# A four-layer kernel: fusion stage reordered with two further products a batch, a convolution moved, chunk products parted

## The reference

```python
q = short_conv_silu(hidden @ Wq, conv_q_w)          # causal convolution of 4 taps, then silu; k and v alike
beta = sigmoid(hidden @ Wb)
# delta rule in chunks of 32 tokens; q, k l2-normed, v and kb = k scaled by beta
attn = -(kb @ k^T) * strict_lower                   # per chunk, 32 x 32
for i in range(1, 32):                              # inverse of (1 - attn), row by row
    attn[i, :i] += attn[i] @ attn[:, :i]
u, w = (attn + eye) @ v, (attn + eye) @ kb
# scan over the 16 chunks:
a_loc = (q_i @ k_i^T) * incl_lower
u_i = u_i - w_i @ S;  o_i = q_i @ S + a_loc @ u_i;  S = S + k_i^T @ u_i
# multi-scale causal convolutions of 3, 15 and 31 taps on v, mixed per head and over channels
ms_out = (concat(conv3, conv15, conv31) @ kernel_mix_w) @ channel_mixer_w
# fusion
feat = concat(hidden, mean|ms_out|, mean|delta_out|, mean|v|)          # 128 + 3 x 4
logits = gelu(feat @ fusion_w1 + b1) @ fusion_w2 + b2                  # 3 per head
wts = softmax(logits)
o = wts0 * ms_out + wts1 * delta_out + wts2 * v
o = o * rsqrt(mean(o * o) + 1e-5) * o_norm_w                           # per head
out = o @ Wo
```

## Time and profile before

| | us |
|---|---|
| median of 3 runs (lowest, highest) | 2881.85 (2876.45, 2889.88) |
| profiled execution | 2890.78 |
| its span | 2889.2 |
| PE busy / DVE busy / ACT busy | 2125.6 / 1844.0 / 1167.1 |
| chunk inputs, 2109.7 to 2303.7 | 194.0 |
| solve and convolution, to 2409.9 | 106.2 |
| chunk products, to 2513.9 | 104.0 |
| serial scan, to 2542.2 | 28.3 |
| fusion, to 2680.3 | 138.1 |

### The profile page before, as it was taken

The page is one execution under the profiler, slowest core; times in us unless marked ns, Lnnn a source line. Parts: engine busy times, 40 slices in busy tenths (PEclk is TensorE's granted clock), DMA queues, the critical chain, the costliest instruction groups (busy, mean ns, idle before and its releaser), DMA issues. The chain is left out here.

```text
span 2889.2 us, 44054 instructions
## 1 busy us (share of the span) xinstructions
PE 2125.6 (74%) x15996; PEld 1090.1 (38%) x15996; DVE 1844.0 (64%) x2951; ACT 1167.1 (40%) x2397; POOL 426.7 (15%) x575
## 2 busy tenths in 40 slices
PE   4476778732538768888868766997778797678798
PEld 3011113421328612222235211886533344555454
DVE  6688887656844387878624588332555495856565
ACT  3699994310002136666643322233433101135433
POOL 3000000000551122222210341113500000000100
PEclk9788889855769969999977777998989799867799
DMA  8512110000345512222100000221112312200000
GB/s 289 103 23 44 22 22 1 14 9 0 105 142 154 147 31 39 51 48 39 27 13 0 21 31 9 98 91 41 42 53 75 102 70 71 67 4 1 22 1 30
DMA packets 146759, 155.28 MB, mean 54 GB/s; under 512 B 53136, under 2 KB 122338, under 8 KB 146586
## 3 DMA queue, kind: packets, MB, share of 16 engines
q1 hardware_dynamic: 131936, 119.71, 16.1%
q0 software_dynamic: 12928, 25.47, 3.6%
q10 hardware_dynamic: 1728, 7.87, 0.7%
HBM read 87.29 MB, written 68.55 MB: 54 GB/s over the span
## 5 line engine op out<-in xcount | busy, mean ns | idle before, releaser
L786 DVE TENSOR_REDUCE a_nmax<-a_first 128x2 f32<-128x1024 f32 x256 | 307.3, 1219 | 87.7 <-PE a_first L883 71.2
L381 ACT ACTIVATE a_E<-a_scores,a_nmax 128x512 f32<-128x512 f32 x512 | 343.3, 726 | 21.7 <-DVE a_nmax L340 21.4
L864 ACT ACTIVATE a_E<-a_scores 128x512 f32<-128x512 f32 x512 | 278.2, 597 | 159.3 <-PE a_scores L897 141.8
L340 DVE TENSOR_REDUCE a_nmax<-a_scores 128x2 f32<-128x1024 f32 x256 | 300.3, 1217 | 37.0 <-PE a_scores L398 35.5
L398 PE MATMUL a_scores<-a_Vh,a_Kh 48*128 48x512 bf16 x512 | 113.7, 461 | 132.4 <-ACT a_E L381 101.4
L897 PE MATMUL a_scores<-a_Qh,a_Kh 51*128 51x512 bf16 x512 | 143.1, 398 | 51.5 <-ACT a_E L864 39.1
L409 PE MATMUL a_out<-a_E,a_QS 128*32 128x512 f32 x1024 | 165.9, 727 | 2.7 <-DVE a_QS L350 2.6
L883 PE MATMUL a_first<-a_Kh,a_Qh 48*128 48x512 bf16 x512 | 122.2, 419 | 34.6 <-DVE a_nmax L786 23.9
L1885 PE MATMUL a_ps_q<-a_yT,a_selI 32*128 32x512 f32 x128 | 101.7, 885 | 57.5 <-DVE a_state L1943 34.1
L910 PE MATMUL a_out<-a_E,a_V 128*32 128x512 f32 x1024 | 143.0, 632 | 0.4 <-POOL a_V L720 0.2
L398 PEld LDWEIGHTS a_scores<-a_Vh,a_Kh 48*128 48x128 bf16 x512 | 24.8, 96 | 304.2 <-ACT a_E L381 218.3
(11 more groups left out here) (464 smaller groups left out, 4644.4 us busy)
## 6 DMA issues: line engine op xcount, KB each, us to landing
f_up<-in_L_up SPq DMA_DIRECT2D x32, 256.0 KB, 2.9
slots<-zeros ACTq DMA_DIRECT2D x12, 640.0 KB, 15.4
a_rows_k<-a_parts SPq DMA_DIRECT2D x16, 384.0 KB
a_Kh<-a_rows_k SPq DMA_DIRECT2D x16, 384.0 KB, 5.8
a_Vh<-a_rows_v SPq DMA_DIRECT2D x16, 384.0 KB, 9.4
a_Qh<-a_rows_q SPq DMA_DIRECT2D x32, 192.0 KB, 4.6
a_Kh<-a_rows_k SPq DMA_DIRECT2D x32, 192.0 KB, 5.1
f_xe<-slots SPq DMA_DIRECT2D x40, 128.0 KB, 2.0
```

Of the source, the lines that this page charges most:

```text
L340: v.tensor_reduce(nmax[:, rd % 2, r1, :, q], ps_s[u % 3][:], AX.X, ALU.max, negate=True).then_inc(S["max_ready"], 1)
L381: m = a.activation(E[:, u % NE, x], ps_s[u % 3][:, x], ACT.Exp, bias=nmax[:, rd % 2, r1, x, q:q + 1], accum_out=Z[:, rd % 2, r1, x, q:q + 1])
L786: v.tensor_reduce(out, ps_f[u % 2][:], AX.X, ALU.max, negate=True).then_inc(S["max_ready"], 1)
L864: a.activation(E[:, u % NE, x], ps_s[x][:], ACT.Exp, scale=SCALE).then_inc(S["exp_ready"], 1)
```

## The change

- `attention3`: G stays allocated through `chunk_scan3`; `eye` is loaded with the first ring loads.
- `chunk_inputs3`: `quads` is parted into `quads_a` and `quads_l`, `masks` into `mask_a` and `mask_l`. The two `sums` products go to 32 partitions each (0 to 31, 32 to 63) instead of adding up in 8; `spread` reads the reciprocals from these two groups of 32.
- `solve_and_convolve3`: PE convolves 6 batches (`CONV3`); the turned copies MT are done by ACT.
- `chunk_scan3`: the 15 early taps of batches 6 and 7 are done here, two taps a step (`taps_of`); ACT issues the loads of q, all at the start; `ps_c` has one buffer instead of two.
- `fusion3`: all engines follow one schedule (`turns`), in which a batch passes through six turns of the loop; branches and o are held for three batches. The two hidden products from the features read rows 0 to 31 and 32 to 63 of FT, which holds the features twice. Two products of the identity by XT are added a batch, into `ps_h`, where the next products overwrite them. The weighted sum isn't divided by the sum of the weights; the square of that sum scales the 1e-5 in the norm instead.
- The weights of layer 0 are freed before layer 2.

```diff
@@ chunk_inputs3, tensor @@
                     for n in range(2):
-                        m = pe.matmul(ps_b[0:8, :], hm8[:, n], sq[:, n], start=(n == 0), stop=(n == 1))
+                        m = pe.matmul(ps_b[32 * n:32 * n + 32, :], hm[:], sq[:, n], start=True, stop=True)
...
-                        m = pe.matmul(ps_n[:, n], sp8[:, n], rs[:], start=True, stop=True)
+                        rows = slice(32 * n, 32 * n + 32)
+                        m = pe.matmul(ps_n[:, n], sp8[rows], rs[rows], start=True, stop=True)
...
+                def quads_a(b):
                     pe.wait_ge(S["kb_ready"], b + 1)
+                    pe.wait_ge(S["a_masked"], b)
+                    quads(b, ps_a, kb[:], y[:, b % 2, 1]).then_inc(S["a_done"], 1)
+                def quads_l(b):
+                    pe.wait_ge(S["normed"], b + 1)
+                    pe.wait_ge(S["l_masked"], b)
+                    quads(b, ps_l, y[:, b % 2, 1], y[:, b % 2, 0]).then_inc(S["l_done"], 1)
...
                     proj(b, 2)
                     if b:
-                        quads(b - 1)
+                        quads_a(b - 1)
                     sums(b)
                     if b + 1 < NB:
                         proj(b + 1, 0)
+                    if b:
+                        quads_l(b - 1)
+                    if b + 1 < NB:
                         proj(b + 1, 1)
                     spread(b)
@@ chunk_inputs3, vector @@
                     if b:
-                        masks(b - 1)
+                        mask_a(b - 1)
                     gated(b, 2)
                     v.wait_ge(S["roots_ready"], b + 1)
                     v.reciprocal(rs[:], nrm[:]).then_inc(S["rs_ready"], 1)
...
                     v.tensor_tensor(vb[:], VT[:, b, PAD3:PAD3 + T], beta[:], ALU.mult)
+                    if b:
+                        mask_l(b - 1)
                     v.wait_ge(S["spread_done"], b + 1)
@@ solve_and_convolve3 @@
-                v.drain()
-                for t in range(NG):
-                    v.tensor_copy(MT[:, t], M[:, t].rearrange("p c e -> p e c")).then_inc(S["solved"], 1)
...
-                for b in range(NB):
+                for b in range(CONV3):
+                    if b == CONV3 - 2:
+                        a.wait_ge(S["inverted"], 1)
+                        for t in range(NG):
+                            a.copy(MT[:, t], M[:, t].rearrange("p c e -> p e c")).then_inc(S["solved"], 1)
                     a.wait_ge(S["ms_done"], b + 1)
@@ chunk_scan3 @@
-                        sp.dma_start(AQ[:, b, 1].rearrange("p n c -> p (n c)"), spill["q"][b]).then_inc(S["q_loaded"], 16)
+                    for b in range(NB):
+                        a.dma_start(AQ[:, b, 1].rearrange("p n c -> p (n c)"), spill["q"][b]).then_inc(q_loaded[b], 16)
...
+                    def taps_of(i):
+                        b, j = CONV3 + i // 8, i % 8
+                        if j == 0 and b > CONV3:
+                            pe.wait_ge(S["ms_read"], b - CONV3)
+                        for s in range(2 * j, min(2 * j + 2, MIXED3)):
+                            m = pe.matmul(ps_m[:], G[:, s], VT[:, b, PAD3 - s:PAD3 - s + T], start=(s == 0),
+                                          stop=(s == MIXED3 - 1))
...
                             solve(i + 1)
+                        taps_of(i)
                         step_matrices(i)
@@ fusion3 @@
+        def turns(i):
+            return [b if 0 <= b < NB else None for b in (i + 2, i + 1, i, i - 1, i - 2, i - 3)]
...
+                    for c in range(2):
+                        pe.matmul(ps_h[:, c], g.ident[:], g.XT[:, b], start=True, stop=True)
                     for c in range(2):
                         pe.matmul(ps_h[:, c].rearrange("f (r p) -> f r p", r=R), W1x[:, c * 128:(c + 1) * 128],
                                   by_row(g.XT[:, b]), start=True, stop=False)
                     pe.wait_ge(S["FT_ready"], b + 1)
                     for c in range(2):
-                        m = pe.matmul(ps_h[:, c], W1f[:, c * 128:(c + 1) * 128], FT[:], start=False, stop=True)
+                        rows = slice(32 * c, 32 * c + 32)
+                        m = pe.matmul(ps_h[:, c], W1f[rows, c * 128:(c + 1) * 128], FT[rows], start=False, stop=True)
```

More of the change, by code:

```diff
@@ L2476, in attention3, with load_ring @@
             chunk_inputs3(nc, g, consts, consts_loaded, VT, G, MK2, spill, mats)
-            kw.ctx.close()
+        MS, OT = k.sb("a3_MS", [C, NB, T]), k.sb("a3_OT", [C, NB, T])
+        kr = Core(nc, ExitStack())
+        with kr.ctx:
+            D = kr.sb("a3_D", [C, NB, T])
+            ring = [kr.sb(f"a3_{n}", [128, RING3, 2, T]) for n in ("lka", "lvk")]
+            ring_loaded = nc.alloc_semaphore("a3_ring_loaded")
+            def load_ring(sp):
+                for b in range(RING3):
+                    load_chunks3(sp, spill, ring, b, ring_loaded)
+                sp.dma_start(eye[:], w["L3_eye32"]).then_inc(ring_loaded, 16)
             solve_and_convolve3(nc, g, VT, G, taps, MS, D, mats, invs, load_ring)
-        OT = k.sb("a3_OT", [C, NB, T])
-        chunk_scan3(nc, g, w, OT, spill, invs, VT, taps, D, MS, MK2, ring, ring_loaded)
+            chunk_scan3(nc, g, OT, spill, invs, VT, taps, D, MS, MK2, G, eye, ring, ring_loaded)
         fusion3(nc, g, w, VT, MS, OT)
+CONV3 = 6
+RING_LOADS = (2 * 3 + 1) * 16
 RING3 = 3
@@ L2616, in _ @@
                         gate(b + 1)
-                quads(NB - 1)
+                quads_a(NB - 1)
+                quads_l(NB - 1)
             @block.scalar
@@ L3096, in _ @@
-                turn_out(NB - 1)
-                project(NB - 1)
+                for i in range(-2, NB + 2):
+                    b_in, b_hid, b_sum, b_norm, b_out, b_add = turns(i)
+                    if b_in is not None:
+                        turn(b_in, 0)
+                        turn(b_in, 1)
+                    if b_hid == 0:
+                        pe.wait_ge(S["loaded"], NLD)
+                    if b_hid is not None:
+                        turn_features(b_hid)
+                    if b_sum is not None:
+                        logits(b_sum)
+                    if b_in is not None:
+                        turn(b_in, 2)
+                    if b_out is not None:
+                        turn_out(b_out)
+                    if b_hid is not None:
+                        hidden(b_hid)
+                    if b_out == 0:
+                        pe.wait_ge(S["wo_ready"], 1)
+                    if b_out is not None:
+                        project(b_out)
@@ L3150, in _ @@
-                out_turned(NB - 1)
+                for i in range(-2, NB + 2):
+                    b_in, b_hid, b_sum, b_norm, b_out, b_add = turns(i)
+                    if b_in is not None:
+                        branch(b_in, 0)
+                        branch(b_in, 1)
+                    if b_hid is not None:
+                        features(b_hid)
+                    if b_norm is not None:
+                        roots(b_norm)
+                    if b_sum is not None:
+                        exponentials(b_sum)
+                    if b_in is not None:
+                        branch(b_in, 2)
+                    if b_out is not None:
+                        out_turned(b_out)
+                    if b_hid == 0:
+                        a.wait_ge(S["loaded"], NLD)
+                    if b_hid is not None:
+                        hidden(b_hid)
+                    if b_sum is not None:
+                        squares(b_sum)
@@ L3152, in _, with features @@
             @block.vector
             def _(v):
[L3154 to L3155 removed]
+                def features(b, n):
+                    if n == 0 and b:
                         v.wait_ge(S["F_turned"], b)
[L3157 to L3161 removed]
```

331 lines of the change are left out of this document (158 added, 173 removed).

## The result

| | before | after |
|---|---|---|
| median, us | 2880.9 (4 runs) | 2806.8 (4 runs, 2799.7 to 2814.1) |
| ratio | | 0.974, interval 0.970 to 0.978 |
| profiled execution, its span | 2890.8, 2889.2 | 2799.7, 2798.1 |
| chunk inputs | 194.0 | 157.1 (-36.9) |
| solve | 106.2 | 85.8 (-20.4) |

The five stages give -73.6 us, the medians -74.1. The two spans differ by 91.1: another 16.0 us arise ahead of the chunk inputs (which start at 2093.7 instead of 2109.7) and 1.5 us behind the fusion, in stages whose instructions the change leaves alone. That they and the medians give the same sum is in part chance.

What follows compares the result with a forecast made beforehand. Each stage has its own bound: TensorE lacking instructions in the chunk inputs, TensorE in the solve, both engines in chunk products, half clock and waits in fusion. Terms -34 - 20 - 3 - 15 = -72 gave 2810 us, range 2788 to 2845.

Steps and rivals of the forecast that it cites:

- the four terms: Predicted changes by stage: chunk inputs -34 us, solve -20, chunk products -3, fusion -15.
- The first two terms: Chunk inputs -34 us by parted products and shorter sums and spread; solve -20 us by moved convolution and copies.
- The instruction theory: Chunk inputs: TensorE's "issue" holes in the second half of `quads`, 21.0 us, are a lack of instructions; parting removes them.
- rival 1: Chunk inputs: holes not for want of instructions, only sums and spread shorten, -6 instead of -34, total 2838 us; 12%.
- twice at worst: Solve: ACT's four MT copies take 1.1 us each as on VectorE, or twice that at worst, under the taps.
- 1 to 2 us: Chunk products: delay from ACT issuing eight q loads, 0.67 us each, before its first copy; 1.5 in the sum.
- I count nothing for them but half a block: Chunk products: the 60 added convolution passes, 26 us in all, fall into instruction holes and cost only 2 us.
- Rival 3: Chunk products: the convolution's passes lie in the open, +23 us instead of -3, total 2836 us; 6%.
- under 1 us each: Chunk products: at steps 6, 10 and 14 `convolve` waits for VectorE's addition because `ps_c` is single.
- The mechanism that I named first: Fusion: the FT wait and the wait for a branch copy go; VectorE and ACT stay below TensorE's 12.1 us.
- my bound at full clock: Fusion: a period of 11.6 us if the clock is full everywhere; 12.6 was taken, with some half clock.
- since the stretch of dense passes grows: Fusion: dense passes grow from 6 to 7.5 us of the period, the reason given for taking 12.6 us.

Runs made afterwards that it cites:

- runs 2 to 4: Changed kernel, product halves joined again: alone (stage 178.8 us); with six overwritten products between (12.0 us longer still); with half the products, twice as wide (10.4 below the changed kernel's).
- run 5: Changed kernel with the eight q loads back on the sync queue, each behind its batch's inverses: chunk products 108.1 us, ratio to the kernel before 0.9705.
- Run 6: Changed kernel with all eight batches' convolution in the solve: solve 105.7 us, chunk products 105.6, ratio to the kernel before 0.981.
- runs 8 to 10: Changed kernel without the fusion's further products, q loads on the sync queue: twice with `convolve` at every second step (chunk products 120.0, 113.4 us), once without that move (108.8).
- run 1: Changed kernel without the two overwritten identity products a batch in the fusion: periods 9.7 us, stage 11.4 us shorter, ratio to the kernel before 0.9726.
- run 7: Kernel before with only the two overwritten identity products a batch added to its fusion: stage 158.8 us instead of 138.1.

## Why the prediction was right, and where a step was not

2810 predicted, 2806.8 measured, inside the range of 2788 to 2845. Three of the four terms had the right sign. The two that were off, by +12.8 and -11.2 us, cancelled: that the sum came within 3.2 us is luck. The first two terms were right in mechanism and size.

*Chunk inputs, -34 predicted, -36.9 measured.* The seven cycles take 119.93 us, 119.7 predicted, with the wait for the squares 1.05 where 1 was said, sums 1.05 (0.95), spread 1.13 (1.0). The instruction theory is shown by runs 2 to 4. The rule of the Trainium skill ("Runtime: NRT & Kernel Launch", Instruction fetch mechanics), by which the fetch is hidden, doesn't hold here: 20.5 us of "issue" go to 0.0 with half the instructions. My price for rival 1 was wrong though: joined halves leave -15.2, not -6. Sums and spread save 0.83 and 0.85 us a batch, 13.4 over eight; my own terms for them, 0.85 and 0.9, give 14, and nothing in the prediction leads from there to 6.

*Solve, -20 and -20.4.* ACT's copies took 1.95 us each, near the end that I had called twice at worst, and lay under the taps as said: they end at 2322.75, the taps at 2336.47. (VectorE's own copies took 0.99 us each, not 1.1.)

*Chunk products, -3 predicted, +9.8 measured: the sum failed here.* By its own terms:
- "1 to 2 us" for ACT's eight q loads in front of the stage. I priced what they hold up on ACT, 0.67 us each, and not what their 2 MB hold up on the way. The first copy of `ps_u` came at 10.6 us instead of 5.1; run 5 gives 5 of these back.
- "I count nothing for them but half a block": 101.3 us of steps instead of 93. Rival 3 took all of the passes as open, I none, since the 2 us of that half block are named and don't stand in the sum (3.6 + 1.5 + 93 + 2.9 = 101). Run 6 has 9.4 us of them on the path.
- The tail was 1.9 us, 2.9 predicted. The 9.7 us of waits for q on VectorE did go, but bought only the tail's shortening from 6.3 us, since TensorE sets the steps: VectorE now waits 27.6 us for `ps_o`.
- The waits for the single `ps_c`, "under 1 us each", were some 1.6 each (4.7 in three), and in runs 8 to 10 the stage got no shorter, rather longer, with them away.

First copy, steps and tail, 5.5 + 8.3 - 1.0, are the whole miss of 12.8 us.

*Fusion, -15 predicted, -26.2 measured.* The mechanism that I named first holds: FT and branch waits gone, TensorE the bound. I took 12.6 a period and measured 11.0; my bound at full clock was 11.6. The step that failed is "since the stretch of dense passes grows": the further products are no part of the gain. Without them the stage is 11.4 us shorter (run 1), and in the old order they cost 20.7 (run 7). Everything else in the stage together is worth -37.6 us, and gives back most of the clock (0.88 in run 1, 0.66 before), as TensorE hardly waits in the cycle any more. In those 37.6 us TensorE's busy time falls by 23.9 and its idle time by 13.7. Of the busy time 6.6 us are the feature products on their two row groups (16.6 us, 10.0 in run 1); order, row groups and the undivided sum weren't run apart.

## What to carry to other kernels

In this kernel idle time "issue" among hundreds of tiny products was a want of instructions. Where you see it, put long products between them, or fewer, wider ones in their place, and don't count on a wait that you remove there: it may come back as "issue". Passes put into such holes are neither free nor in the open: here some two thirds were hidden. Before you add work to hold a clock up, take away the waits by order alone and look at the clock again, and price a load by what shares its way, not only by its issue.

## What the hardware showed that I had not expected

- After an instruction packet ends, a TensorE that had run dry goes on 1.3 to 1.5 us later (14 holes), and packets that follow each other closely start some 3.8 us apart (24 in the chunk products of run 6).
- A copy of 128x1024 with a transposed read takes ACT 1.95 us (7.78 for four) and VectorE 0.99 (3.95 for four).
- Four passes whose moving operand is read with a stride (`by_row`) take 3.76 us, four of the identity by the same tile read straight 1.88, both behind each other in a batch after, where the granted clock is 1.00. The timeline of TensorE there:

```profile
2484.81 1.88 PE L3077 MATMUL a3f_ps_h<-XT,ident 128*128 128x512 f32 x4
2486.53 3.76 PE L3079 MATMUL a3f_ps_h<-XT,a3f_W1x 128*128 128x512 f32 x4
```

  The strided passes hardly feel the clock: in the kernel before they take 3.93 us where the granted clock is 0.50 (2562.3 to 2566.0). In run 7 the identity's four passes take 3.48 us at 0.53 and the strided four behind them 3.78 at 0.95. Over the whole fusion stage the strided passes take 31.2, 30.2 and 30.1 us at clocks of 0.66, 0.73 and 0.93. So the largest group of the fusion had nearly nothing to win from a higher clock, which the further products were meant to bring.

- Two products in different column groups (`sums`) or row groups (`spread`) of the array, with different moving data, run together: four passes in 1.05 and 1.13 us.
